# Layer 0's decay matrices by running products in place, and its SiLUs as one ScalarE operation each

## The reference

```python
dA = jnp.exp(dt * A)                       # one decay per token and head
dBx = einsum('blhp,bln,blh->blhpn', x, Bmat, dt)
state = state * dA_t + dBx_t               # scan over tokens
y = einsum('lbhpn,bln->blhp', states, Cmat) + D * x
y = rmsnorm(y * silu(z), norm_gate_w) @ W_out
h = silu(h @ mlp_w1 + mlp_b1) @ mlp_w2 + mlp_b2   # layer 0 only, behind the mixer
```

## Time and profile before

| | us |
|---|---|
| runs (3) | 1697.21, 1696.18, 1690.65 |
| median | 1696.18 |
| profiled execution, its own time | 1692.49 |
| its span, first to last instruction | 1690.8 |
| PE busy in the span | 1556.4 (92%) |
| DVE / ACT / POOL busy | 1122.5 / 768.9 / 706.8 |
| mean granted TensorE clock | 0.954 |

### The profile page before, as it was taken

One profiled execution on the slowest core, in us unless ns is written; L12 is line 12 of the kernel. 1 busy time (PEld: TensorE's weight loads), 2 busy tenths in 40 slices (PEclk: granted clock), 3 DMA queues, 4 the chain that ended last, 5 costly groups with the idle time before them and its releaser, 6 DMA issues.

```text
span 1690.8 us, 23271 instructions
## 1 busy us (share of the span) xinstructions
PE 1556.4 (92%) x7307; PEld 1073.6 (63%) x7307; DVE 1122.5 (66%) x2583; ACT 768.9 (45%) x1562; POOL 706.8 (42%) x751
## 2 busy tenths in 40 slices
PE   4989999999999999999878888899988999999996
PEld 3555756757566575756554455555557888988985
DVE  4868577684866758576248888987875654555542
ACT  1425162451625425162316555566545555555562
POOL 1555536364563655536311222233232553443452
PEclk7979989999999999999889999999999999999998
DMA  6000020101001010010122111111102442433432
GB/s 200 0 13 13 1 63 1 50 12 38 25 0 59 4 50 12 0 51 1 38 88 90 35 63 62 60 58 52 50 25 85 102 100 65 85 74 86 96 51 25
DMA packets 66855, 84.00 MB, mean 50 GB/s; under 512 B 12360, under 2 KB 57296, under 8 KB 66768
## 3 DMA queue, kind: packets, MB, share of 16 engines
q1 hardware_dynamic: 54480, 65.86, 12.1%
q0 software_dynamic: 12288, 17.05, 6.0%
HBM read 57.53 MB, written 25.36 MB: 49 GB/s over the span
## 4 chain that ended last, share of the span: by engine, by line
PE 26%; issue 13%; POOL 7%; DVE 3%; ACT 1%; DMA 1%; PEldq 0%; POOLq 0%; DVEq 0%; PEld 0%; SPq 0%
PE bank L2060 25%; POOL yb L920 2%; POOL Xs L912 2%; POOL ry L928 1%; PE bank L2435 1%; DVE am L1874 1%; POOL out L976 1%; POOL ry L925 0%; POOL xg L951 0%; DVE hits L1780 0%; DVE E L1896 0%; DVE yb L1907 0%; DVE u L1874 0%; DMA xg<-rows_d,IDX 0%; DMA hT<-xnT_d 0%
## 5 line engine op out<-in xcount | busy, mean ns | idle before, releaser
L2015 DVE TENSOR_TENSOR aml<-m0big,amh 128x512 fp32r<-128x512 f32 x128 | 88.0, 688 | 175.4 <-ACT amh L1320 175.3
L976 POOL DMA_INDIRECT out<-EW,IDX x64 | 105.1, 1642 | 223.5 <-DVE EW L2000 208.9
L1315 ACT ACTIVATE m0big<-bank,eb 128x512 f32<-128x512 f32 x128 | 87.9, 687 | 161.3 <-PE bank L2060 145.9
L2060 PE MATMUL bank<-w2h,amh 128*128 128x256 f32 x512 | 147.9, 289 | 0.0
L2060 PE MATMUL bank<-h2T,EW 128*128 128x512 f32 x320 | 146.8, 596 | 0.3
L2060 PE MATMUL bank<-w2h,aml 128*128 128x256 f32 x512 | 144.8, 283 | 0.0
L2060 PE MATMUL bank<-w2l,amh 128*128 128x256 f32 x512 | 144.7, 283 | 0.0
L2060 PEld LDWEIGHTS bank<-Xdt,E 128*128 128x128 f32 x768 | 95.7, 201 | 56.7 <-issue 56.7
L2060 PE MATMUL bank<-EW,am 128*128 128x256 f32 x512 | 115.8, 379 | 1.2 <-DVE am L1639 1.2
L920 POOL TENSOR_TENSOR yb<-yb,zs 128x512 f32<-128x512 f32 x32 | 40.5, 1267 | 171.9 <-DVE yb L1911 171.8
L1110 ACT ACTIVATE am<-bank,b 128x512 f32<-128x512 f32 x64 | 43.9, 686 | 148.0 <-PE bank L2060 148.0
(11 more groups left out here) (327 smaller groups left out, 3810.0 us busy)
## 6 DMA issues: line engine op xcount, KB each, us to landing
EW<-in_e_w SPq DMA_DIRECT2D x16, 1024.0 KB, 5.5
m0big<-dA_d SPq DMA_DIRECT2D x16, 512.0 KB, 4.7
xin<-in_L_attn_x SPq DMA_DIRECT2D x8, 512.0 KB
xp<-in_L_attn_x SPq DMA_DIRECT2D x8, 512.0 KB, 3.7
rows_d<-xo SPq DMA_DIRECT2D x8, 512.0 KB, 3.0
x_d<-xb SPq DMA_DIRECT2D x8, 512.0 KB, 4.0
xnT_d<-nT SPq DMA_DIRECT2D x8, 512.0 KB, 4.4
out<-x SPq DMA_DIRECT2D x32, 128.0 KB, 1.7
```

Of the source, the lines that this page charges most:

```text
L976: g.indirect_dma_start(out=out_rows, out_offset=bass.IndirectOffsetOnAxis(ap=IDX[:, 4 * u + c:4 * u + c + 1], axis=0), in_=ye[:, q, c, :], ...
L1315: a.activation(am2[:, j % 2, :], bank[j % 2][:, :], ACT.Gelu, bias=eb1[:, u // 2, j:j + 1]).then_inc(gelu_sig.sem, 1)
L2015: v.tensor_tensor(aml[:, j % 4, :], am2[:, j % 2, :], amh[:, j % 4, :], ALU.subtract).then_inc(am_low.sem, 1)
L2060: return t.matmul(out_, lhsT, rhs, start=first, stop=last)
```

## The change

Decays of layer 0. The logs of the decays (already in `dtv`) are transposed by PE (`LOGT`), ACT takes their exp, which gives dA as 32 rows of 128, SP stores these to DRAM and loads them back broadcast over 128 partitions, one load of 512 KB for each chunk (`load_decays0`), and DVE runs two scans of 128x512 over each, in place (`scans`). Each chunk has a buffer of its own (`E0`). POOL's `terms`, PE's `decay_sums`, ACT's exps and the mask on G are gone. G and B^T have two banks in turn (`GP0`, `BTP0`), the second in the bank that `decay_sums` used; DVE reads G there. The logs are summed for the other decays (`decay_log_sums`) right after the projections, before `h2T`, and their exp (`decay_exp`) stands before the SiLUs on ACT.

SiLUs of layer 0. Convolution, z and `up` each have one ACT operation with `ACT.Silu`; the DVE products and the halved weights are gone. The addition of D*x moves from POOL to DVE, ahead of the wait for `INTRA`. SP's loop over the steps is written out in Python.

```diff
+            def store_decays(i):
+                sp.wait_ge(own, 2)
+                s0.dA.wait_ge(sp, i, 1)
+                for c in range(CH):
+                    s0.dA_loaded[c].wait_ge(sp, i, 0)
+                sp.dma_start(dA0_d.rearrange("c (h t) -> (c h) t", t=P), dAT0[:, :]).then_inc(s0.dA_stored.sem, 16)
+            def load_decays0(i, c):
+                if c == 0:
+                    s0.dA_stored.wait_ge(sp, i, 16)
+                s0.intra_full.wait_ge(sp, i - 1, c + 1)
+                sp.dma_start(E0[c], dA0_d[c].partition_broadcast(P)).then_inc(s0.dA_loaded[c].sem, 16)
...
-            with sp.Fori(1, STEPS - 2) as b:
+            for b in range(1, STEPS - 2):
                 load_x(b + 2)
+                decays_of(b + 1)            # store, loads 0 and 1
                 load_residual(b + 1)
+                later_decays_of(b + 1)      # loads 2 and 3
                 store_back(b)
...  ScalarE
+            def conv_silu(L, s, i, j):
+                    a.activation(s.u_buf[:, blk, :], s.u_buf[:, blk, :], ACT.Silu).then_inc(s.xc.sem, 1)
...
             def decay_exp(L, s, i):
+                s.dA_stored.wait_ge(act, i, 0)
+                a.activation(dAT0[:, 1:P], LOGT[:, 1:P], ACT.Exp).then_inc(s.dA.sem, 1)
...
+                raw(L, s, i, 4)
+                decay_exp(L, s, i)
                 for j in range(5):
-                    conv_tanh(L, s, i, j)
-                    if j == 0:
-                        raw(L, s, i, 4)
+                    conv_silu(L, s, i, j)
...
-                a.activation(am[:, k, :], p[:, :], ACT.Identity, bias=b1[:, k:k + 1]).then_inc(act2.sem, 1)
-                ins = a.activation(tt[:, k % 2, :], p[:, :], ACT.Tanh, bias=b1[:, k:k + 1])
+                a.activation(am[:, k, :], p[:, :], ACT.Silu, bias=b1[:, k:k + 1]).then_inc(am_sig.sem, 1)
...  VectorE
+            def scans(L, s, i, c):
+                s.dA_loaded[c].wait_ge(dve, i, 16)
+                for j in range(L.segs):
+                    e = E0[c][:, 512 * j:512 * (j + 1)]
+                    v.tensor_tensor_scan(e, e, ID0, 0.0, ALU.mult, ALU.add).then_inc(s.E.sem, 1)
...
+                    v.tensor_tensor(e3, e3, GP0[q].unsqueeze(1).to_broadcast([P, 4, P]), ALU.mult).then_inc(s.M.sem, 1)
...
+                s.xd.wait_ge(dve, i, c + 1)
+                ch.put(v.tensor_tensor(yb[:, q, :], yb[:, q, :], XD[:, q, :], ALU.add))
...  order in step0
                     start(L, s, f)
+                    scans(L, s, f, 0)
                     chunk(L, s, f, 0, dve0)
+                    scans(L, s, f, 1)
                 for c in range(CH):
                         if c + 1 < CH:
                             chunk(L, s, f, c + 1, dve0)
                         sums(L, s, f, c, dve0)
                         if c:
                             mixed0(s, f, c - 1)
+                        if c + 2 < CH:
+                            scans(L, s, f, c + 2)
...  TensorE
+                last = t.transpose(LOGT, s.dtv_buf[:, 1, 0:m], ident[:, :])
...
                 for j in range(1, 5):
                     in_proj(L, s, i, j)
+                decay_log_sums(L, s, i)
...
-                decay_sums(0)
```

More of the change, by code:

```diff
@@ L262, in program @@
         hits1 = hits[:, :, :].rearrange("p t e -> p (t e)")
-        L1T = [R[:, P * k:P * (k + 1)] for k in range(7)]
+        L1T = [dA0b[:, P * k:P * (k + 1)] for k in range(7)]
+        E0 = (dA0a[:, :], dA0b[:, :], E[:, 0, :], E[:, 1, :])
         wq, wrT, lvT, woT = (am[:, k, :].rearrange("p (k n) -> p k n", k=KD) for k in range(4))
@@ L337, in program @@
         pool_prep = sem("pool_prep")
+        own = sem("identity_rows_ready")
         phase = sem("phase")
@@ L855, in step0 @@
                     back_rms(b, 0, CH - 1, poolb)
-                if f is not None:
-                    terms(L, s, f, 0, pool0)
                 if b is not None:
@@ L1021, in raw @@
                 a.activation(xbuf[:, blk, L.halo:L.halo + T], p[:, :], ACT.Copy).then_inc(s.xb.sem, 1)
-            def conv_tanh(L, s, i, j):
+            def conv_silu(L, s, i, j):
+                blk = (j - 1) % 5
                 s.u.wait_ge(act, i, j + 1)
-                s.xc.wait_ge(act, i, j)
-                a.activation(th[:, j % 2, :], s.u_buf[:, (j - 1) % 5, :], ACT.Tanh).then_inc(s.th.sem, 1)
+                if j == 0:
+                    n, cp = L.state, L.cpart
+                    a.activation(s.Ct_buf[0:n, :], s.u_buf[cp:cp + n, 4, :], ACT.Silu).then_inc(s.xc.sem, 1)
+                    a.activation(s.u_buf[0:n, 4, :], s.u_buf[0:n, 4, :], ACT.Silu).then_inc(s.xc.sem, 1)
+                else:
+                    a.activation(s.u_buf[:, blk, :], s.u_buf[:, blk, :], ACT.Silu).then_inc(s.xc.sem, 1)
             def decay_exp(L, s, i):
@@ L1067, in chunk @@
                 p = front_wait(act, L, s, i, f"z{c}")
[L1068 to L1076, removed]
+                s.yg.wait_ge(act, i, c - 1)
+                a.activation(zs[:, q, :], p[:, :], ACT.Silu).then_inc(s.zs.sem, 1)
                 p = front_wait(act, L, s, i, f"xt{c}")
@@ L1357, in _, with scale @@
             count = 0
-            def scale(out_, factor, second=None):
+            def scale(out_, factor):
                 nonlocal count
-                v.tensor_scalar(out_, out_, factor, second, ALU.mult,
-                                ALU.mult if second is not None else ALU.bypass).then_inc(prepped, 1)
+                v.tensor_scalar(out_, out_, factor, None, ALU.mult, ALU.bypass).then_inc(prepped, 1)
                 count += 1
             def mixer_weights(L, w):
-                if L.tree:
-                    scale(w["conv"][:, :, :], 0.5)
                 for k in range(CH):
@@ L1715, in step0 @@
                     dveb.end()
+            v.tensor_copy(ID0.rearrange("p (h t) -> p h t", h=4),
+                          ident[:, :].unsqueeze(1).to_broadcast([P, 4, P])).then_inc(own, 1)
+            v.memset(dAT0[:, 0:1], 0.0).then_inc(own, 1)
+            dve.wait_ge(own, 2)
             norm(0)
@@ L2154, in chunk @@
                 n = L.state
-                s.bs.wait_ge(pe, i, c)
+                if c >= 2:
+                    s.M.wait_ge(pe, i, (c - 1) * L.segs)
                 if c == 0:
-                    s.ex.wait_ge(pe, i, 1)
-                if not L.tree:
-                    if isinstance(i, int) and i == 0 and c == 0:
-                        pe.wait_ge(ph0, 2)
-                    cnt_sig.wait_ge(pe, i, c)
-                    mm(CNT, ones[:, :], cnt[:, :])
-                mm(GP, s.u_buf[0:n, 4, cols(c)], s.Ct_buf[0:n, cols(c)])
-                t.transpose(BTP[:, 0:n], s.u_buf[0:n, 4, cols(c)], ident[0:n, 0:n]).then_inc(s.g_full.sem, 1)
-                for j in range(1, L.segs):
-                    decay_sums(j)
+                    s.dA.wait_ge(pe, i, 1)
+                mm(GP0[q], s.u_buf[0:n, 4, cols(c)], s.Ct_buf[0:n, cols(c)])
+                t.transpose(BTP0[q][:, 0:n], s.u_buf[0:n, 4, cols(c)], ident[0:n, 0:n]).then_inc(s.g_full.sem, 1)
             def recur(L, s, i, c):
@@ L2240, in step0 @@
                 if f is not None:
-                    decay_log_sums(L, s, f)
                     chunk(L, s, f, 0)
```

128 lines of the change are left out of this document (41 added, 87 removed).

## The result

The changed kernel takes 1708.89 us (median of 8 runs, 1702.76 to 1711.56), the kernel before 1695.52 (8 runs beside them, 1690.65 to 1697.48). Ratio 1.0076, 95% interval 1.0065 to 1.0088: slower by 0.8%, where I forecast 1667 and gave "slower" 0.09. The profiled execution took 1710.8 us, its span is 1709.1.

A forecast was written before the change was run, and what follows sets the result against it. PE's own list was taken to bound layer 0's steps. Steps 1 to 7: head +5.1, chunks -8.1, -3.0 each, -21; step 0 -6; total -27 on 1692.49 is 1665.5, median put at 1667, range 1660 to 1680.

The forecast's parts named there:

- Part 2: DVE in the chunks: scans cost nothing, with 39.3 us of work in 42, 93% busy, just under PE.
- one of 0.76: PE's only standstill in a steady step's chunks, 0.76 us for DVE's `x`, counted as gone.
- Part 5: Clock behind the head's wait: falls from 1.00 to 0.50, bounds 0 and 3.4 us, taken as 2.6 per step.
- step 0 worth nothing rather than 6: Step 0: PE waits 3.35 and 3.65 us for the chain over DVE; gain between 0 and 12, taken as 6.
- Part 1: PE's decay matmuls go: 7.3 us per step; with the wait for `x`, chunks 8.1 us less.
- Part 3: Decays' way over DRAM on SP: ten us of cover, cost 0; with the cover gone, a us per us.
- Part 4: ACT in the head: exps, table load and two Silus before the h2T copy; PE stands 3.2 us instead of 0.97.
- rival B: Every ACT table switch in the steps also costs the skill page's drain of 1380 ns: 1677 us; chance 0.08.
- A: The head's wait costs no clock, 1649 us, or is hidden altogether, 1631 us; chance 0.26.
- C: DVE takes over as the bound in the chunks, 48 us against 49.4 before: 1720 us, slower; chance 0.12.
- D: Decay loads come late, sharing engines with the step's stores; 3 us late are 1688; chance 0.09 with the rest.
- the head's +5.1: Head of steps 1 to 7: +3.1 wait, -0.59 log sums moved away, +2.6 clock, +5.1 us per step.

The follow-up runs named there:

- k5: The changed kernel with one wait added on DVE: scans of chunk c+2 start only after POOL's gated product of chunk c; 1661.81 us, ratio 0.9797.
- k1: The changed kernel with ACT's two h2T copies moved right behind the decay exps, ahead of the table load and Silus; 1669.77 us, ratio 0.9836.
- k12: k3 with ACT's yT copy moved ahead of the dt exp and one unread matmul added per step at its end; 1627.06 us, ratio 0.9588.
- k8: k3 with three unread 128x512 matmuls added per step, two ahead of PE's wait for xo, one ahead of the router's; 1638.30 us.
- k7: The changed kernel with the SiLUs of before (tanh on ACT, product on DVE), so scans and two G banks alone; 1724.86 us, ratio 1.0163.
- k3: The changed kernel with both moves: h2T copies ahead of the table load, all eight scans ahead of chunk 0; 1638.72 us, ratio 0.9636.
- k2: The changed kernel with all eight scans of a step and all four decay loads ahead of chunk 0; 1666.88 us, ratio 0.981.
- k9: k8 with ACT's last-chunk square and yT copy moved ahead of the next step's small dt exp; 1640.46 us, ratio 0.9668.
- k11: k3 with ACT's yT copy moved ahead of the dt exp, without any added matmul; 1638.85 us.

## Why the prediction was wrong

**Part 2 is the step that failed:** "I cost it at nothing". I asked only whether DVE keeps ahead of PE. In steps 1 to 7 it does: it stood still 11 to 12 us before chunk 0, the D*x addition took 0.68 us where I took 0.995, 55 of layer 0's 64 scans took 1.19 to 1.23 us (the nine others, all of `dA0b`, 1.87 to 1.99), and the mask product is at 0.68 as forecast. What I didn't ask is what the scans do to POOL. I had the rule in hand, from the Trainium skill ("SBUF — State Buffer", Who interferes with whom), and read it one way: scans "exposed", so perhaps 1.85 us long. The same section says that what collides is an exclusive lock, and that the order of issue decides who is blocked. At the place that mattered DVE isn't slowed and POOL is: 3.82 us against 1.27, and 1.27 again as soon as DVE waits (k5). The trace agrees with the lock: the product is longer by the scans' length. With the order it agrees at one place and not at the other: at 460.04 POOL began 0.25 us ahead and DVE lost, at 468.45 POOL's product began 0.43 us ahead by the trace and lost all the same (the profile's times on POOL are rough). In its own list POOL has air, but the product of chunk 0 is wanted by PE's `y_turned` at once. So a wait of 1.38 us came where I had taken one of 0.76 away.

**Its price was the clock.** The chunks fell short by 47.4 - 41.2 = 6.2 us per step: 1.4 is the wait, 4.8 the half clock behind it, and the two kinds of step in k1 (42.69 and 47.6) show the same split. Part 5 knew this price and I asked for it in one place only, the head. The bound that I drew from the earlier trace rows, that a wait of 0.97 us leaves the clock alone, gave me no reason to fear 1.4, had I seen it. Seven steps of 6.2 are 43 us, and 42 lie between 1667 and 1709. That they agree so closely is partly luck, for smaller misses about cancel: the heads 1.1 each better than forecast, step 0 worth nothing rather than 6 (there DVE did hold PE up, 3.08 us, with the half clock behind it; and of the two waits that I took for the chain's, the one of 3.65 us is for `h`, the next step's norm, and is 4.04 us in the changed kernel).

**Part 1** was right in size: with nothing in the way the chunks are 41.2 us (k12), forecast 41.3. **Part 3** was right in its cost: the load of dA0a took 4.1 us, the first scan waited for it (1.7 to 2.9 us in steps 1 to 7, 3.9 in step 0), and PE never waited for a load of decays. **Part 4** was right: wait 3.13 (forecast 3.2), two loads per step, the second in ACT's idle time (k8 shows one at 484.64 whose exp starts at 487.89), and no drain: the Silu starts 1.29 us after the load does, in this step too (438.15, 439.44), so rival B falls: the drain that the Trainium skill ("ScalarE: Activation LUTs", What ACT_TABLE_LOAD costs) adds to a load isn't borne out here. **Part 5** was right in kind for the head and somewhat high in size: the head grew by 4.0 where parts 4 and 5 have 5.1. Of that 2.2 is the wait, so the clock cost about 1.8 in place of 2.6.

**Rivals.** A falls, since the clock was lost. C had the sign and the wrong mechanism: in steps 1 to 7 PE's chunks did not wait for DVE. C's price (1720) lies by the kernel with the old SiLUs (k7, 1725), in which DVE does set the pace, but that is its mechanism in a kernel that it wasn't priced for, and the closeness is chance. D (late decays) falls: PE never waited for them. No rival asked who shares a resource with the engine that gets more work. And I had accepted the head's +5.1 as a price of the change, where one move on ACT takes all of it away and some of the old wait too (k1).

## What to carry to other kernels

When work moves to an engine, ask what it blocks as well as whether the engine has the time: here two scans on DVE tripled one product on POOL that PE wanted next. A short wait of PE has to be priced with the clock behind it (here 3.3 to 4.9 us behind a wait of 1.4, in 12 of 14 cases), and each place where one may appear needs that price. Before accepting a wait, look at what stands in order ahead of the operation that ends it; two copies moved up on ACT and the scans moved up on DVE turned 0.8% slower into 3.6% faster (k3).

## What the runs showed of the hardware that I had not expected

- The length of a wait alone doesn't tell whether the clock falls. The wait of 1.30 to 1.38 us in the chunks was followed by the fall from 1.00 to 0.50 in all seven steps of the changed kernel, and in five of seven in k1. The one of 3.13 to 3.22 us in the head was followed by it in seven of seven, but in k2 and in k5 in six. At the step's end 0.57 to 0.70 us of waiting beside thin matmuls (128x8, 128x12) is followed by it in every version without added matmuls there, while 0.97 us in the head of before is not the earlier trace rows, nor 1.37 us between the 128x512 matmuls of k9's head. In k8 PE waited for yT 1.45 to 2.02 us in six steps, and the clock fell in two. So what else decides it is open. The longest of k8's, and the clock behind it:

```profile
303.34 1.99 PE L2046 MATMUL bank<-m0big,yT 128*128 128x256 f32 x8 [2.02 <-ACT yT L1115]
```

```profile
303.00:306.00 3.00, 2.66 (x10) 2.01 (x11) 2.37 (x13) 2.82 (x9) 1.58 (x4) 1.00 0.49 158
```

- A slow spell may cover waits: at the step's end it shows 3.4 us lost per step, and the cheapest way of removing it gave 11.8 us in seven (k12 against k11), since ACT's copies come no earlier and PE waits for them instead. A spell's loss in the records isn't what its removal gives.
- Two scans of 128x512 with both inputs in SBUF hold back a product of POOL that by the trace has already begun, for as long as both scans last and not for one of them: 2.55 us more for 2.32 us of scans. A scan that starts 0.25 us behind a product of POOL is itself held up, 1.87 us in place of 1.20. Which of the two loses can't be told from the starts in the trace.
